# Key spreading moved from VectorE to ScalarE in two attention stages, tokens loaded in eight groups, and semaphores handed back at three places instead of nine

## The reference

```python
x = x + _L0_xattn_ref(_layernorm(x, axis=-1), ctx_768, L0_xattn_q_w, ...)   # first stage
...
scores = einsum(q, k) * hd ** -0.5          # q: tokens, k: context rows (L0) or the tokens themselves (L3)
probs = jax.nn.softmax(scores, axis=-1)
out = jnp.einsum('bhqk,bkhd->bqhd', probs, v).reshape(B, T, d)
return out @ Wo + bo
```

## Time and profile before

| | us |
|---|---|
| median of three runs (2621.17 to 2627.2) | 2624.64 |
| the profiled execution | 2621.33 |
| its span, first to last instruction | 2619.5 |

### The profile page before, as it was taken

The page is one execution under the profiler, slowest core; times in us unless marked ns, Lnnn a source line. Parts: engine busy times, 40 slices in busy tenths (PEclk is TensorE's granted clock), DMA queues, the critical chain, the costliest instruction groups (busy, mean ns, idle before and its releaser), DMA issues. The chain is left out here.

```text
span 2619.5 us, 41956 instructions
## 1 busy us (share of the span) xinstructions
PE 2026.6 (77%) x15215; PEld 1499.1 (57%) x15215; DVE 1548.1 (59%) x3817; ACT 1024.6 (39%) x1945; POOL 1111.0 (42%) x967
## 2 busy tenths in 40 slices
PE   5887699599999876700794788688589788869997
PEld 3666499476766633300683556466467466647775
DVE  6995522465666474477344885511497699935553
ACT  3775244244444430133331444233144355623332
POOL 3443463444333217586786863362575200012221
PEclk9996899799999988955896876799699799979998
DMA  3000378300000046965772100332231000010000
GB/s 103 2 2 19 123 221 216 107 11 13 10 11 5 1 156 213 358 207 183 238 219 63 25 13 1 117 91 72 90 117 41 1 2 2 2 37 1 0 0 33
DMA packets 122014, 204.57 MB, mean 78 GB/s; under 512 B 19416, under 2 KB 66433, under 8 KB 118027
## 3 DMA queue, kind: packets, MB, share of 16 engines
q1 hardware_dynamic: 97966, 139.93, 16.0%
q0 software_dynamic: 23872, 62.29, 8.9%
HBM read 137.34 MB, written 64.82 MB: 77 GB/s over the span
## 5 line engine op out<-in xcount | busy, mean ns | idle before, releaser
L2941 PE MATMUL banks<-ident,L1o_hid 128*128 128x128 f32 x288 | 42.2, 291 | 163.5 <-DMA L1o_hid<-mixed,L1f_token_of 152.8
L324 POOL TENSOR_TENSOR L1x_soft<-L1x_soft,L1x_rinv 128x616 f32<-128x616 f32 x64 | 77.8, 1216 | 210.8 <-DVE L1x_rinv L257 210.6
L1778 PEld LDWEIGHTS banks<-L3f_w,L3f_hT 128*128 128x128 f32 x1024 | 126.5, 195 | 30.6 <-issue 29.8
L2941 PEld LDWEIGHTS banks<-ident,L1o_hid 128*128 128x128 f32 x288 | 33.7, 148 | 170.5 <-DMA L1o_hid<-mixed,L1f_token_of 153.8
L1769 PE MATMUL banks<-L3f_xT,L3f_w 128*128 128x512 f32 x256 | 129.6, 637 | 0.0
L1800 DVE SCALAR_TENSOR_TENSOR L3f_acc<-banks,L3f_gates,L3f_acc 128x128 f32<-128x128 f32 x256 | 72.0, 344 | 95.9 <-PE banks L1778 95.3
L1789 ACT ACTIVATE L3f_hT<-banks,L3f_b 128x512 f32<-128x512 f32 x128 | 87.2, 686 | 104.3 <-PE banks L1769 101.4
L1778 PE MATMUL banks<-L3f_w,L3f_hT 128*128 128x128 f32 x1024 | 127.2, 278 | 0.0
L723 POOL TENSOR_TENSOR L0x_soft<-L0x_soft,L0x_rinv 128x1232 f32<-128x1232 f32 x32 | 71.9, 2247 | 98.4 <-DVE L0x_rinv L658 98.4
L2574 ACT ACTIVATE L0e_hT<-banks,L0e_w 128x256 f32<-128x256 f32 x156 | 69.1, 474 | 87.2 <-PE banks L2617 87.2
L2268 POOL DMA_INDIRECT L0e_rows<-xn_rows,L0f_token_of x78 | 77.9, 998 | 56.7 <-PE banks L2608 35.3
(11 more groups left out here) (550 smaller groups left out, 6041.1 us busy)
## 6 DMA issues: line engine op xcount, KB each, us to landing
hidden<-L1h_hid SPq DMA_DIRECT2D x24, 768.0 KB, 8.1
L0e_w<-in_L0f_w SPq DMA_DIRECT2D x39, 320.0 KB, 3.7
L0e_w<-in_L0f_w SPq DMA_DIRECT2D x39, 258.0 KB, 3.3
mixed<-L1m_out SPq DMA_DIRECT2D x32, 256.0 KB, 2.1
L3x_keys<-L_keys SPq DMA_DIRECT2D x6, 1232.0 KB
xn_rows<-L1f_xn_all SPq DMA_DIRECT2D x3, 2048.0 KB
L1h_w<-in_L1f_w SPq DMA_DIRECT2D x24, 256.0 KB, 6.7
L1h_b<-in_L1f_b SPq DMA_DIRECT2D x24, 256.0 KB, 8.6
```

Of the source, the lines that this page charges most:

```text
L324: pool.tensor_tensor(tile, tile, rinv[n % 2][:, :].unsqueeze(2).to_broadcast([P, U, NK]), ALU.mult).then_inc(probs_ready, 1)
L1778: last = pe.matmul(y_bank[e % 2][:, b * P:(b + 1) * P], hT[e % 2][:, c, b * P:(b + 1) * P], w2[:, e, c, :], start=(c == 0), stop=(c == FC ...
L2941: last = pe.transpose(turn_bank[k % 4][:, c * P:(c + 1) * P], hid[e % N][:, q, c * P:(c + 1) * P], net.ident[:, :])
```

## The change

Three edits.

The spread keys are made by ScalarE. For each head place j (no longer for each batch) one ACTIVATE takes the keys of all four batches from PSUM, with scale `diag[:, j]` and bias `bk_diag[:, j]`, and writes to `kbd` with gaps between the batches. `bk_diag` = `diag` x `bk` is made once by VectorE. The elements per instruction are as before (128x308 in L0x, 128x512 in L3s), and so is the number of instructions, four a turn. Their places are at the end of ScalarE's iterations b = 1 and b = 2.

The start block keeps only VectorE's fills. L0x's own block loads: the first four batches of tokens, then `ident`, `diag`, the eight tiles of L0x and the context on one semaphore, then the other seven groups of tokens, each with its own semaphore, then what was loaded beside L0x before, with `index64` added. VectorE's variances wait for their own group. VectorE, TensorE and GpSimd wait for the semaphore of the tiles.

Six of nine releases are gone; those behind the first experts, ahead of the latent stage and ahead of the last wide attention L3x remain.

```diff
-def packed_attention_stage(nc, net, spec, w, later=None):
+def packed_attention_stage(nc, net, spec, w, later=None, first=None):
...
+        bk_diag = sb("bk_diag", [P, 4])
...
         def variances(dve, t):
+            if first:
+                dve.wait_ge(x_loaded[t], 16)
...
-        def take_keys(dve, t, bs):
-            kps = prep_bank[:, 0:4 * NK].rearrange("p (b k) -> p b k", b=4)
-            dve.wait_ge(k_ps, t + 1)
-            for b in bs:
-                last = dve.scalar_tensor_tensor(
-                    kbd[t % 2][:, b, :, :], kps[:, b:b + 1, :].to_broadcast([P, 4, NK]), bk[:, 0:1],
-                    diag[:, :].unsqueeze(2).to_broadcast([P, 4, NK]), ALU.add, ALU.mult)
-            if 3 in bs:
-                last.then_inc(k_out, 1)
+        def take_keys(act, t, heads_of_strip):
+
+            kps = prep_bank[:, 0:4 * NK].rearrange("p (b k) -> p b k", b=4)
+            act.wait_ge(k_ps, t + 1)
+            for j in heads_of_strip:
+                last = act.activation(kbd[t % 2][:, :, j, :], kps, ACT.Identity, scale=diag[:, j:j + 1],
+                                      bias=bk_diag[:, j:j + 1])
+            if 3 in heads_of_strip:
+                last.then_inc(k_out, 1)
...
             @block.sync
             def _(sp):
+                def load_tokens(t):
+                    sp.dma_start(x[:, 4 * t:4 * t + 4, :], first["x"][:, 4 * t:4 * t + 4, :]).then_inc(x_loaded[t], 16)
+
+                load_tokens(0)
+                for tile, src in first["loads"]:
+                    sp.dma_start(tile[...], src).then_inc(first_loaded, 16)
+                for t in range(1, NTURN):
+                    load_tokens(t)
                 for tile, src in later:
                     sp.dma_start(tile[...], src).then_inc(kept_loaded, 16)
...
         def _(dve):
             variances(dve, 0)
+            if first:
+                dve.wait_ge(first_loaded, 16 * len(first["loads"]))
+            dve.tensor_scalar(bk_diag[:, :], diag[:, :], bk[:, 0:1], None, ALU.mult).then_inc(bias_masked, 1)
...
             normalize(dve, 0)
-            take_keys(dve, 0, range(4))
...
-                if b == 1 and t + 1 < NTURN:
-                    take_keys(dve, t + 1, range(2))
-                if b == 2 and t + 1 < NTURN:
-                    take_keys(dve, t + 1, range(2, 4))
...
         def _(act):
             take_tokens(act, 0)
+            act.wait_ge(bias_masked, 1)
+            take_keys(act, 0, range(4))
             take_queries(act, 0)
...
+                if b == 1 and more:
+                    take_keys(act, t + 1, range(2))
+                if b == 2 and more:
+                    take_keys(act, t + 1, range(2, 4))
                 if b == 3 and more:
                     take_values(act, t + 1)
...
         def _(pe):
+            if first:
+                pe.wait_ge(first_loaded, 16 * len(first["loads"]))
...
-        loaded = net.sem("start_loaded")
+        first = [(net.ident, t["ident"]), (net.diag, t["diag"])] + first + [(net.context, t["ctxT"])]
+        later.append((net.index64, t["index64"]))
         with nc.Block() as block:
-            @block.sync
-            def _(sp):
-                sp.dma_start(net.x[:, :, :], t["x"]).then_inc(loaded, 16)
...
-                sp.wait_ge(loaded, 16 * (5 + len(first)))
-
...
-        packed_attention_stage(nc, net, spec("L0x", 16), w0, later=later)
-        net.release_semaphores()
+        packed_attention_stage(nc, net, spec("L0x", 16), w0, later=later, first=dict(x=t["x"], loads=first))
```

More of the change, by code:

```diff
@@ L607, in packed_attention_stage @@
         bias_ps, bias_ready, recip_ready = sem("bias_ps"), sem("bias_ready"), sem("recip_ready")
+        bias_masked = sem("bias_masked")
         ones_ready = sem("ones_ready")
@@ L806, in packed_attention_stage @@
         if later:
-            kept_loaded = sem("kept_loaded")
+            kept_loaded, first_loaded = sem("kept_loaded"), sem("first_loaded")
+            x_loaded = [sem(f"x_loaded{t}") for t in range(NTURN)]
             @block.sync
             def _(sp):
+                def load_tokens(t):
[5 more added lines that the diff above has]
+                    load_tokens(t)
                 for tile, src in later:
@@ L825, in _ @@
                 pool.wait_ge(bias_ready, 1)
+            if first:
+                pool.wait_ge(first_loaded, 16 * len(first["loads"]))
             add_bias(pool, 0)
```

## The result

The changed kernel takes 2607.9 us (median of seven runs, 2604.8 to 2613.3) against 2624.6 before; the ratio is 0.9943 with a 95% interval of 0.9924 to 0.9963. The medians differ by 16.7 us and the ratio is worth 15; 16 were forecast (2609 us). The profiled execution has a span of 2607.1 us against 2619.5, 12.4 less; for that execution 15.8 were forecast.

The account below looks back on a forecast made before the run. No engine bounds the whole: loads at the start, a TensorE-ScalarE loop close behind VectorE in L0x, late VectorE in L3s. 4.7 + 0.3 + 5.1 + 5.7 = 15.8 us off 2621.3 gives 2605.5, median 2609 us; range 2603 to 2615, wider 2598 to 2619.

Parts of the forecast that it names:

- Start, 4.7 forecast: Kernel start: context issued by about 7.8 us, seen at 13.2, first normalization at 13.3 instead of 18.0; bounds 2.7 to 6.2.
- The figure of the Trainium skill: Start: about 2 us fixed plus bytes over 436 GB/s, context there at 11.6, saving 1.6 us more; forecast preferred its own.
- L0x, 0.3 forecast: First packed attention: 0.8 us gained at b = 3, less 0.2 for late `k_out` and 0.3 for turn 0's keys.
- The late `k_out`: L0x, b = 2: ScalarE's key pair releases `k_out` about 0 to 0.1 us late, seven times, costing 0.2 us.
- L3s, 5.1 forecast: Second packed attention: `shift` ends 4.32 us after `values` instead of 5.28, b = 3 iteration 8.55 instead of 9.51, five turns.
- that term of 0.4: L3s, turn 0: its b = 3 iteration falls from 8.49 to 8.12 us, counted as 0.4 of the saving.
- the upper bound of 7.3: L3s: most that could be saved, in us, if `shift` falls to 3.89 after `values` everywhere; lower bound 3.
- Releases, 5.7 forecast: Between stages: six releases removed take 6.5 us, less about 0.8 of clears done later; bounds 4 to 6.5.
- What ScalarE pays: Key activations on ScalarE: 1.15 us a pair in L0x, 1.46 in L3s, each set slower by a tenth or two.
- the slower one: Rival, keys in ScalarE's loop: excess lengthens it, 2643 us; slower from about 0.9 us an activation; 4 in 100.
- The clock's effect: Rival, TensorE's clock: shifted stages lengthen or cut a low stretch; thirty us more low, half hidden, gives 2616 us; 12 in 100.
- The meetings: Rival, where stages begin with loads: waits cover the releases' meetings, only half might be lost, 2612 us; 8 in 100.

Follow-up runs that it names:

- The two repeats: The unaltered change run again: 2648.5 us, ratio 0.9944, on a chip where the kernel before takes 2662.8; a third time elsewhere, 2608.1 us, ratio 0.9933.
- The early: The changed kernel with the context issued by SyncE as second load instead of twelfth, on the same semaphore: 2604.5 us, ratio 0.9929.
- the two-semaphore kernel: Context-early kernel with variances ahead of the add, plus L0x's loads on two semaphores, context and rest awaited only by TensorE: 2597.4 us, ratio 0.9907.
- the variances moved: The changed kernel with VectorE's variances ahead of the add at b = 2: 2603.0 us, ratio 0.9915; in L3s alone 2602.2 us, ratio 0.9923.
- The doubled keys: The changed kernel with every ScalarE key activation also written to a spare tile, four activations a visit instead of two: 2623.7 us, ratio 0.9999.

## Why the prediction was right

**Start, 4.7 forecast, 5.1 measured.** The issue of the context ended at 6.95 instead of 7.8: the 7.8 was counted from the old list, which holds one issue of 1.19 us (`diag`), and none came here. VectorE saw it at 12.7 instead of 13.2. The two repeats have their first normalization at 14.1 and 13.0, so the term is 4 to 5 us from one execution to the next. The early and the two-semaphore kernel confirm the model of what was waited for, and correct it in one point: small tiles behind a large one land after it, one by one. The figure of the Trainium skill that the forecast set beside its own (DMA: Bandwidth & Descriptors, Anatomy of one DMA) is given there for transfers that GpSimd issues, and these go out from SyncE; it had the context at 11.6, which was 1.1 too early. The instruction list behind it costs nothing: the second variances had their tokens.

**L0x, 0.3 forecast, 2.1 measured** (from the first normalization to L0n, the release apart: 206.1 to 204.0 us; 199.5 and 200.9 in the two repeats). This term was wrong in size, and most of what came is the clock. Of the sum's own items b = 3 gave the 0.8, and b = 0 fell from 5.92 to 5.83, another 0.5 that I had not seen. The late `k_out` cost nothing at the step, 6.59 in all later turns. Two effects of over 3 us nearly cancel in this profile. The first: TensorE's matmuls took the long times of the low level until about 49 us, where before had left it by 47.6, though the granted clock is shown as 1.00 there, and a step of 6.6 us took 9.74:

```profile
43.05 1.94 PE L791 MATMUL banks<-L0x_probsT,L0x_vals 77*32 77x128 f32 x32 [0.67 <-ACT L0x_probsT L702]
52.79 1.08 PE L791 MATMUL banks<-L0x_probsT,L0x_vals 77*32 77x128 f32 x32 [0.72 <-ACT L0x_probsT L702]
```

The second: at the end the granted clock held, where before had fallen. Windows of before, then of after, the clock in the third column from the right:

```profile
214.00:218.00 4.00, 4.00 (x44) 3.54 (x35) 0.09 (x1) 1.46 (x3) 0.00 (x0) 0.50 0.00 0
...
200.00:216.80 16.80, 12.13 (x186) 9.53 (x184) 6.33 (x10) 9.77 (x19) 5.62 (x3) 1.00 0.00 1
```

The last two steps took 4.16 each, 3.4 us less than the 5.09 and 6.65 of before:

```profile
210.02 1.08 PE L791 MATMUL banks<-L0x_probsT,L0x_vals 77*32 77x128 f32 x32 [0.67 <-ACT L0x_probsT L702]
214.18 1.08 PE L791 MATMUL banks<-L0x_probsT,L0x_vals 77*32 77x128 f32 x32 [0.67 <-ACT L0x_probsT L702]
```

The late rise belongs to this execution: the other two profiles of the change have 6.59 at that step. The clock that holds at the end is not; it came with the keys in each of them.

**L3s, 5.1 forecast, 4.9 measured** (262.0 to 257.1 us). Lag and step came out within 0.02 us. Turn 0 was 8.46 instead of the 8.12 forecast: that term of 0.4 failed. It was replaced by turn 6, which went from 8.12 to 7.89. So 8.12 was not the floor that TensorE and ScalarE set, as the forecast took it to be: VectorE's keys stood in turn 6 as well. With the variances moved, all turns but turn 0 are at 7.9, and from the first `values` to the last the stage has won 8.8 us in all, more than the upper bound of 7.3.

**Releases, 5.7 forecast, 5.8 measured.** The three left take 1.4, 1.7 and 1.2 us with every engine in them; nine took 10.1. Clears did grow with what they clear, 0.7 of 0.8.

**What ScalarE pays.** The forecast has each set slower by a tenth or two on ScalarE. In L0x that holds (four in turn 0 take 2.11 us against VectorE's 1.88). In L3s its own figures, 1.46 a pair against twice 0.74, don't say so, and the rows show 2.78 against 2.73.

**The sum.** The four parts come to 5.1 + 2.1 + 4.9 + 5.8 = 17.9 us, and the profiled execution lost 12.4: 5.5 went elsewhere, most of it in the stages between 1231 and 1842 us, which no edit explains. The median came within 1 us of its forecast all the same, partly by luck: the profiled execution was 3.4 us slower than forecast, but it lies 1.0 above its median, where the forecast had put it 3.3 below.

**The rivals.** The doubled keys show that the slower one had its turning point close by: one more pair of activations in ScalarE's loop and the change is worth nothing. The clock's effect is real, both signs, 3 us at a time. The meetings: behind three of the six that went, no load is waited for, and the next stage's first work comes 1.4, 1.3 and 1.1 us sooner after the last one's, the whole meeting. Behind the other three stands a routing that waits for a load issued after the meeting. There the time from the last logits to VectorE's first instruction is 5.1 to 5.6, 5.6 to 6.4 and 4.6 to 4.8 us with the meeting (three profiles) and 4.2 to 5.1, 4.8 to 5.7 and 3.6 to 4.9 without: most of it was won, and at the third, behind L2x, only some 0.4 of 1.0. So this rival is right in small part.

## What to carry to other kernels

An engine that is 97% busy is not the bound until another turn, where it has less to do, shows the same step shorter. Compare the same step of the loop at two loads of the engine: the difference is a first figure of what relief can bring, here 0.2 us a turn in one stage and 1.4 in the other (1.6 in the end, since the lighter turn still held some of its work). Before moving work to an idle engine, find the gap it lands in and measure it against the work; then look at what in the relieved engine's list waits, with other work queued behind it, since turning two entries round brought another 3.8 us where taking 22 us of work away had brought 5. Do it stage by stage: the same turn lost time in L0x, where another engine waits for the entry that was put second. And let the first instructions wait for the few tiles that they read, not for all.

## What the hardware showed that I had not expected

A small VectorE instruction can be held for as long as GpSimd's. The instruction that adds epsilon to four variances takes 0.17 us in most turns of the kernel before. In L0x of the changed kernel it does so in turn 0 only. It takes 1.18 us in turn 2 and 0.98 in turns 3 to 7, and ends there within 0.05 us of GpSimd's multiplication. The kernel with only the keys moved has the same 0.98, those with only the loads or the releases 0.17: relieved of the keys, VectorE comes to this instruction while GpSimd still multiplies. In turn 1 it took 1.82, beside GpSimd's clearing of a tile:

```profile
15.34 1.82 DVE L629 TENSOR_SCALAR L0x_rstd<-L0x_mean_var 128x4 f32<-128x4 f32 x1
...
15.34 1.80 POOL L843 MEMSET L0x_vals<- 77x2048 f32 x1
```

The last kernel is the change with that MEMSET put ahead of GpSimd's wait for the tiles:

```diff
             invert_root(pool, 0)
+            pool.memset(vals[1][:, :, :, :], 0.0).then_inc(zeroed, 1)
...
             add_bias(pool, 0)
-            pool.memset(vals[1][:, :, :, :], 0.0).then_inc(zeroed, 1)
```

> The changed kernel, and GpSimd clears its second value tile before it waits for the tiles of L0x instead of right behind the bias. In three profiles VectorE's 128x4 TENSOR_SCALAR of turn 1 took 1.82 us and ended with that MEMSET of 1.80. My account: it was held by the MEMSET, so with the MEMSET away from it the same instruction takes 0.17 us, and invert_root of turn 1 starts over 1 us earlier; the time of the kernel doesn't move, since turn 1's normalization isn't waited for. Rival (the stall comes from the loads that run at the time): it stays at 1.8.

```profile
6.88 1.80 POOL L833 MEMSET L0x_vals<- 77x2048 f32 x1
...
15.35 0.17 DVE L629 TENSOR_SCALAR L0x_rstd<-L0x_mean_var 128x4 f32<-128x4 f32 x1
15.60 1.02 POOL L713 TENSOR_TENSOR L0x_rstd<-L0x_rstd,minus_half 128x4 f32<-128x4 f32 x1 [0.19 <-DVE L0x_rstd L629]
```

0.17 us, with the same loads running beside it. So GpSimd held it. The waits beside the multiplication have the same form, but no kernel here moves the multiplication away, and what they cost L0x's loop is not tested. The time of this kernel, two runs at 2643.6 with an interval of 0.9815 to 0.9979, is too coarse to say whether it matters; the first scores stand where they stood. The Trainium skill (SBUF — State Buffer, Who interferes with whom) states it as an exclusive lock held for a whole instruction, by whichever started first, for TENSOR_SCALAR in its fast mode among others, and that reductions never meet it. Here the TENSOR_SCALAR agrees, 1.82 against 0.17; that it was in the fast mode no row shows.
